# Residual stream kept transposed in two feed-forward stages of a fused macaron block

## The reference

```python
x = x + 0.5 * ffn(layernorm(x))
x = x + attn(layernorm(x))        # one head of 128, rotary, causal
x = x + 0.5 * ffn(layernorm(x))   # the same weights again

def ffn(xt):                      # xt: 8192 tokens x 128
    scores = sigmoid(xt @ gate_w.T)            # 16 experts
    idx = top_k(scores + gate_b, 4)
    w = 2.5 * scores[idx] / sum(scores[idx])   # comb: tokens x 16, zero elsewhere
    y = sum over e of comb[:, e] * (silu(xt @ g_e.T) * (xt @ u_e.T)) @ w2_e.T
    return y + (silu(xt @ g_s.T) * (xt @ u_s.T)) @ w2_s.T
```

## Time and profile before

| | before |
|---|---|
| median of 3 executions | 861.89 us (861.54 to 862.0) |
| profiled execution, own time | 863.0 us |
| span, first to last instruction | 861.2 us |
| PE busy | 844.4 us (98%) |
| DVE busy | 694.2 us (81%) |
| ACT busy | 591.2 us (69%) |
| POOL busy | 557.6 us (65%) |
| mean granted PE clock | 0.998 of full |
| HBM read and written | 74.92 MB, 5.24 MB |

### The profile page before, as it was taken

The page is one execution under the profiler, slowest core; times in us unless marked ns, Lnnn a source line. Parts: engine busy times, 40 slices in busy tenths (PEclk is TensorE's granted clock), DMA queues, the critical chain, the costliest instruction groups (busy, mean ns, idle before and its releaser), DMA issues.

```text
span 861.2 us, 18145 instructions
## 1 busy us (share of the span) xinstructions
PE 844.4 (98%) x4506; PEld 709.0 (82%) x4506; DVE 694.2 (81%) x2125; ACT 591.2 (69%) x1215; POOL 557.6 (65%) x519
## 2 busy tenths in 40 slices
PE   8999999999999999999999999999999999999998
PEld 7788888888888876889999998788888888888886
DVE  6888888888888887777776667788888888888885
ACT  5566666666666687777778866766666666666664
POOL 6666666666666678866767762466666666666664
PEclk9999999999999999999999999999999999999999
DMA  3684444455555341222111220445545444444553
GB/s 123 185 233 113 111 111 113 114 126 131 133 122 136 101 114 36 50 51 46 38 40 25 48 49 1 111 124 129 134 124 136 111 111 111 112 112 125 127 134 82
DMA packets 63494, 89.01 MB, mean 103 GB/s; under 512 B 7520, under 2 KB 26208, under 8 KB 63200
## 3 DMA queue, kind: packets, MB, share of 16 engines
q1 hardware_dynamic: 63456, 88.58, 41.3%
HBM read 74.92 MB, written 5.24 MB: 93 GB/s over the span
## 4 chain that ended last, share of the span: by engine, by line
PE 52%; ACT 4%; issue 2%; DVE 2%; POOL 1%; ACTq 0%; DVEq 0%; POOLq 0%
PE bank L1318 47%; PE bank L1628 3%; PE bank L1402 1%; PE bank L1423 1%; ACT prob L740 1%; ACT probT L551 1%; ACT xn L612 1%; ACT qkT L551 1%; ACT xh L551 0%; ACT xn L558 0%; POOL qkT L412 0%; DVE prob L933 0%; DVE X L1214 0%; DVE probT L943 0%; PE bank L1416 0%
## 5 line engine op out<-in xcount | busy, mean ns | idle before, releaser
L412 POOL TENSOR_TENSOR h_l<-probT,h_h 128x512 fp32r<-128x512 f32 x254 | 328.9, 1296 | 202.8 <-ACT h_h L551 202.7
L551 ACT ACTIVATE h_h<-probT 128x512 fp32r<-128x512 f32 (+1 forms) x286 | 179.5, 628 | 72.6 <-DVE probT L943 70.0
L1318 PE MATMUL bank<-xh,w_h 128*128 128x512 f32 x544 | 223.4, 411 | 2.0 <-DVE prob L933 1.9
L586 ACT ACTIVATE bank<-bank 128x512 f32<-128x512 f32 x252 | 146.2, 580 | 103.0 <-PE bank L1318 98.6
L1318 PE MATMUL bank<-xh,w_l 128*128 128x512 f32 x544 | 214.9, 395 | 0.0
L933 DVE TENSOR_TENSOR prob<-bank,qkT 128x512 f32<-128x512 f32 x252 | 173.5, 689 | 50.6 <-ACT bank L586 37.7
L1318 PE MATMUL bank<-xl,w_h 128*128 128x512 f32 x544 | 213.2, 392 | 0.0
L943 DVE TENSOR_TENSOR probT<-prob,bank 128x512 f32<-128x512 f32 x255 | 173.8, 681 | 12.7 <-DVE biased L874 5.0
L1318 PEld LDWEIGHTS bank<-xh,w_h 128*128 128x128 f32 x544 | 102.7, 189 | 23.9 <-DVE prob L933 2.7
L1318 PEld LDWEIGHTS bank<-xh,w_l 128*128 128x128 f32 x544 | 102.5, 188 | 23.9
L1318 PEld LDWEIGHTS bank<-xl,w_h 128*128 128x128 f32 x544 | 102.9, 189 | 19.5
(11 more groups left out here) (117 smaller groups left out, 1332.4 us busy)
## 6 DMA issues: line engine op xcount, KB each, us to landing
qkT<-comb_rows SPq DMA_DIRECT2D x190, 256.0 KB, 5.2
qkT<-comb_rows SPq DMA_DIRECT2D x124, 128.0 KB, 2.9
stage<-stage SPq DMA_DIRECT2D x64, 128.0 KB, 2.4
X<-in_x SPq DMA_DIRECT2D x16, 256.0 KB, 6.2
out_x<-X SPq DMA_DIRECT2D x15, 256.0 KB, 5.8
comb_rows<-combT SPq DMA_DIRECT2D x32, 32.0 KB, 1.8
cos<-in_cos SPq DMA_DIRECT2D x1, 1024.0 KB, 8.3
sin<-in_sin SPq DMA_DIRECT2D x1, 1024.0 KB, 10.7
```

The source lines that it names most:

```text
L412: nc.gpsimd.tensor_tensor(lo, f, hi.bitcast(F32), ALU.subtract).then_inc(done, 1)
L551: return nc.scalar.activation(dst, src, ACT.Copy)
L586: nc.scalar.activation(bank[:, G_BANK[g], :], bank[:, G_BANK[g], :], ACT.Silu).then_inc(silu_done, 1)
L1318: return nc.tensor.matmul(dst, lhsT, rhs, start=start, stop=stop)
```

## The change

The residual of both FFNs is kept transposed (features on partitions) in four buffers `xT`, a ring of 512 tokens each. In the first FFN they are loaded from a transposed copy `x_t` that the host gives; in the second they are made from the rows of `X` by four PE transposes and one ACT copy. The output leaves the kernel transposed and the host turns it. The rows of `X` are still loaded, for the statistics.

The minus mean and the inverse deviation of tile T+3 are written by POOL into two new rows of `comb`; they ride along with the transposition of `comb` and its trip through DRAM, and one more DMA repeats them over 128 partitions (`rows`). POOL adds the minus mean to `xT` (`ffn_center`, 128x512), DVE multiplies by the deviation into bank 7 (`ffn_scale`, 128x512), two tiles ahead. `ffn_xn` and `ffn_xnT` remain for the first two tiles of each FFN. The residual is added by DVE straight from the bank `Y` to `xT`; in the first FFN, PE transposes the sum and ACT copies it into `X` (`ffn_X`); in the second it is stored as it is. The loops have bodies of four tiles, and PE's loop of the second FFN is written out.

```diff
+RING = 4
+TURNS = TILES // RING
@@ SP
+            load(X[:, 2 * NB:3 * NB, :], x_v[:, 2 * NB:3 * NB, :], x_loaded[2])
             load(w13_f[:, early[2], :], w13T[:, early[2], :], w13_loaded[2])
             load(w2_f, w2T, w2_loaded)
-            load(X[:, 2 * NB:3 * NB, :], x_v[:, 2 * NB:3 * NB, :], x_loaded[2])
+            load(X[:, 3 * NB:4 * NB, :], x_v[:, 3 * NB:4 * NB, :], x_loaded[3])
+            for r in range(RING):
+                load(xT[r], x_t[:, TILE * r:TILE * (r + 1)], xT_moved[r])
...
+            def load_xT(T, r):
+                sp.wait_ge(y_ready, T - RING + 1)
+                sp.dma_start(xT[r], x_t[:, bass.ds(TILE * T, TILE)]).then_inc(xT_moved[r], 16)
...
+                if ahead:
+                    wait(sp, xs_done, scaled_count(T + 1, base))
+                    sp.dma_start(rows[:], comb_d[q, NEXP:NEXP + 2, :].rearrange("(a e) t -> a e t", a=1
+                                                                                ).to_broadcast([P, 2, TILE])
+                                 ).then_inc(rows_loaded, 16)
+            def store(T, r):
+                sp.wait_ge(xr_done, T + 1)
+                sp.dma_start(out_t[:, bass.ds(TILE * (T - TILES), TILE)], xT[r]).then_inc(xT_moved[r], 16)
...
+                    for c in range(RING):
+                        comb_rows(4 * k + 2 + c, c % 2)
+                        load_x(4 * k + 6 + c, c % 2)
+                        load_xT(4 * k + 4 + c, c)
...
+                    for c in range(RING):
+                        store(4 * k + TILES + c, c)
+                        comb_rows(4 * k + TILES + 2 + c, c % 2, 0, TILES)
@@ POOL
+            def ffn_rows(T, q):
+                at = slice(NB * q, NB * (q + 1))
+                pool.wait_ge(var_done, ln_count(T))
+                wait(pool, combT_ready, T - 2)
+                nc.gpsimd.tensor_tensor(comb[:, NEXP + 1, :], var_eps[:, at], neg_half[:, at], ALU.pow).then_inc(rstd_done, 1)
+                nc.gpsimd.tensor_tensor(comb[:, NEXP, :], mv[:, at, 0], neg_one[:, at], ALU.mult).then_inc(neg_mean_done, 1)
+            def ffn_center(T, base, turn, c):
+                n = scaled_count(T, base)
+                pool.wait_ge(rows_loaded, 16 * n)
...
+                wait(pool, xs_done, n - 1)
+                nc.gpsimd.tensor_tensor(xc, xT[c], rows[:, 0, :], ALU.add).then_inc(xc_done, 1)
...
-                    elif j == 2 and not last:
-                        ffn_rstd(T + 2)
+                    elif j == 2 and (t is None or t + 3 < TILES):
+                        ffn_rows(T + 3, 1 - q)
+                    if j == 3 and ahead:
+                        ffn_center(T + 2, base, turn + (c + 2) // RING, (c + 2) % RING)
@@ ACT
+            def ffn_xh(T, q, base):
+                act.wait_ge(gate_ready, UNITS * (T - 1))
+                act.wait_ge(xs_done, scaled_count(T, base))
+                copy(xh[q][:], bank[:, T_BANK, :]).then_inc(xh_done, 1)
+            def ffn_xT(T, turn, c):
+                act.wait_ge(xT_ready, turned_count(T))
+                act.wait_ge(xT_moved[c], 16 * turn)
+                copy(xT[c], bank[:, YT_BANK, :]).then_inc(xT_copied, 1)
+            def ffn_X(T, Tx):
+                act.wait_ge(y_ready, T + 1)
+                copy(X[:, tile_blocks(Tx), :], bank[:, YT_BANK, :].rearrange("p (n d) -> p n d", n=NB)).then_inc(x_done, 1)
...
                         ffn_silu(T, q, j)
+                    if j == UNITS - 1 and ahead:
+                        ffn_xh(T + 2, q, base)
...
-                    if j == LAG and not first:
-                        ffn_yT(T - 1, 1 - q)
+                    if base:
+                        if j == 0 and ahead:
+                            ffn_xT(T + 2, turn + (c + 2) // RING, (c + 2) % RING)
...
+                    elif j == PAIRS - 1 and not first:
+                        ffn_X(T - 1, T - 1)
...
-                    elif 0 <= at < NB and not last:
-                        ffn_xn(T + 2, Tx + 2, at)
@@ DVE
+            def ffn_scale(T, base):
+                dve.wait_ge(xc_done, scaled_count(T, base))
+                dve.wait_ge(combT_done, T)
+                nc.vector.tensor_tensor(bank[:, T_BANK, :], xc, rows[:, 1, :], ALU.mult).then_inc(xs_done, 1)
...
+                    nc.vector.scalar_tensor_tensor(xT[c][:, cols], bank[:, Y_BANK[c % 2], cols], 0.5, xT[c][:, cols],
+                                                   ALU.mult, ALU.add).then_inc(xr_done, 1)
...
                     ffn_h(T, q, j)
+                    if j == NB and not first:
+                        residual(T - 1, back)
...
                 ffn_weighted(T, q, PAIRS - 1)
-                if not first:
-                    residual(T - 1, Tx - 1)
                 ffn_h(T, q, PAIRS - 1)
+                    ffn_scale(T + 2, base)
...
                 ffn_h(T, q, PAIRS)
+                    ffn_xl(T + 2, q)
@@ DVE, ffn_start: between ln_apply and ffn_xl(0, 0), and after it
+                dve.wait_ge(x_loaded[1], 16)
+                ffn_stats(1, 1, 1)
+                ffn_stats_wait(1)
+                ffn_mv(1, 1)
+                ffn_var(1, 1)
                 ffn_xl(0, 0)
+                dve.wait_ge(x_loaded[2], 16)
+                ffn_stats(2, 2, 0)
@@ PE
+            def ffn_y(T, c):
+                pe.wait_ge(xr_done, T + 1)
...
+                    ins = nc.tensor.transpose(bank[:, YT_BANK, n * P:(n + 1) * P], xT[c][:, n * P:(n + 1) * P], ident[:])
+            def ffn_xT(T, Tx):
+                pe.wait_ge(attn_done, QB * (Tx // 2 + 1))
+                wait(pe, xT_copied, turned_count(T) - 1)
...
-                if not last:
+                if first:
                     ffn_xnT(T + 1)
+                if base and (t is None or t + 2 < TILES):
+                    ffn_xT(T + 2, T + 2 - base)
...
-                    if j == 4 and not first:
+                    elif j == 6 and not first:
...
+                if start:
+                    with pe.Fori(0, TURNS - 1) as k:
+                        for c in range(1, RING + 1):
+                            ffn_tile(base, k + c // RING, c % RING)
+                else:
+                    for t in range(1, TILES - LAG):
+                        ffn_tile(base, turn + t // RING, t % RING)
```

More of the change, by code:

```diff
@@ L223, in macaron @@
         neg_shift_done = sem("neg_shift_done")
+        rows_loaded = sem("rows_loaded")
+        xc_done = sem("xc_done")
+        xs_done = sem("xs_done")
+        xT_ready = sem("xT_ready")
+        xT_copied = sem("xT_copied")
         xn_done = sem("xn_done")
@@ L425, in ffn_tile @@
+            def ffn_tile(base, turn, c, first_batch=None):
+                T, q = RING * turn + c, c % 2
+                last, t = False, None
+                if isinstance(T, int):
+                    t = T - base
+                    last = t == TILES - 1
+                ahead = t is None or t + 2 < TILES
                 for j in range(UNITS):
@@ L622, in comb_spread, with ffn_tile @@
                                                            ).to_broadcast([P, NB, 2, INTER])).then_inc(spread_copied, 1)
-            def ffn_tile(T, Tx, q, first, last, first_batch=None, start=False):
+            def ffn_tile(base, turn, c, first_batch=None):
+                T, q = RING * turn + c, c % 2
+                first, last, t = False, False, None
+                if isinstance(T, int):
+                    t = T - base
+                    first, last = t == 0, t == TILES - 1
+                start = first and base == 0
+                ahead = t is None or t + 2 < TILES
                 for j in range(UNITS):
@@ L630, in ffn_tile @@
                             attn_hi(FIRST_HI[j], 0, 0)
-                    if j == 0 and not last and not start:
-                        ffn_xh(T + 1, 1 - q)
+                    if j == 0 and first and not start:
+                        opening_xh(T + 1, 1 - q)
                     if j == (7 if start else 6) and not last:
@@ L995, in ffn_tile @@
+            def ffn_tile(base, turn, c, first_batch=None):
+                T, q = RING * turn + c, c % 2
+                first, last, t = False, False, None
+                if isinstance(T, int):
+                    t = T - base
+                    first, last = t == 0, t == TILES - 1
+                start = first and base == 0
+                stats_next = t is None or t + 3 < TILES
+                N, L, Lx, back = T + 1, T + 3, T + 3 - base, (c - 1) % RING
                 if start:
```

420 lines of the change are left out of this document (212 added, 208 removed).

## The result

The changed kernel takes 872.76 us (median; 868.94 to 875.63) where the kernel before takes 861.71 (861.41 to 862.0): ratio 1.0121, 95% interval 1.0105 to 1.0137. It is slower by 11 us; 850.0 was predicted, faster by 12. Two things are in the trace: leaving out what four tiles take too long, the span is shorter by 11.7 us, near the 12.1 predicted; and in these four tiles something that I had given a chance of 0.05 took 17.65 in the profiled execution and some 21 in the middle one.

A forecast was written before the change was run, and what follows sets the result against it. PE, never idle in the FFNs, was taken as the bound. From 861.9 us, transposes -12.2, start +1.1 and end -1.0 sum to -12.1, so 849.8, rounded to 850.0; range 847.0 to 854.2.

The forecast's parts named there:

- the longer loop bodies stall: Rival: four-tile bodies cost an instruction fetch at each of four jumps back, 0 to 12 us, middle 856; chance 0.05.
- Price of the transposes: PE in the FFNs: 0.45 us a group of four transposes, net 27 groups gone, 12.2 us less (11.6 to 12.4).
- DVE at the tile's end: DVE's new scale, 0.68 us, replaces the residual in the end-of-tile cluster; 1.4 us of cover, cost nothing, bound 0.3 a tile.
- the match-replace row: DVE's two-SBUF-input operation in the loop: 160 to 171 ns in all 128 executions, read as no blocking by POOL.
- POOL: POOL in each tile: centering adds 1.29 us, moves the low half of unit 4 by 0.4; covered with 1.2 left.
- DMA: FFN tile loads: `rows` and `xT` land at about 146.5, cover about 1.8 us; likely no cost, up to 1 us once.
- the rival at 879: Rival: the DMA queue becomes the bound, `rows` or `xT` landing late in every tile; 879 us, chance 0.05.
- the one at 858: Rival: DVE's chain at the tile's end passes its 1.4 us by 0.3, 8 us over 27; 858 us, chance 0.07.
- Start: Kernel's start: DVE makes tile 1's statistics before `xl` of tile 0, +1.1 us (ends 0 and 1.4).
- The half-clock stretch: Near the start, PE at 1.2 GHz for some 3.5 us; 1.3 us either way if it vanished or came twice.
- End: Kernel's end: DVE reads `Y` itself, SP issues the store about 0.98 earlier, -1.0 us (0.5 to 1.0).
- Attention: Between the FFNs: extra statistics on DVE, a copy moved from DVE to ACT; 0, bounds -0.5 and +0.5.

The follow-up runs named there:

- experiment 7: Changed kernel, four-tile loops kept, with 110 one-cell memsets on DVE ahead of its first wait for x: 870.34 us, ratio 1.0086.
- experiment 4: Kernel of experiment 1 with each group of four transposes through bank 4 issued twice: 861.12 us, ratio 0.9985 to the kernel before.
- experiment 1: Changed kernel with only DVE's two FFN loops written out (the written-out version, without jumps): 851.3 us against 862.5, ratio 0.9867.
- experiment 11: Kernel before plus, behind all its work, DVE probes of 128x512 in three operand forms, POOL idle then busy: 0.62 us alone, 1.69 and 1.66 beside POOL with two SBUF inputs.
- experiment 2: Kernel before with DVE's loop bodies of four tiles instead of two, leftover tiles written out: 875.29 us, ratio 1.0161.
- experiment 6: Kernel before, DVE's two-tile body padded by 66 one-cell memsets a tile (348 and 347 instructions): 877.52 us, one execution.
- experiment 5: Kernel before, DVE's two-tile body padded by 36 one-cell memsets a tile (288 instructions in the first FFN): 862.06 us, one execution.
- experiment 3: Changed kernel, second FFN's loop loads of comb_b bringing 128 of 512 columns: 869.17 us, one execution.
- experiment 8: Changed kernel with 110 one-cell memsets on DVE behind the first FFN's loop, so only the second loop moves: 870.12 us, ratio 1.0098.
- experiment 9: Kernel of experiment 6 with 88 one-cell memsets ahead of DVE's first wait for x: 892.24 us, one execution.
- experiment 10: Kernel of experiment 6 with 44 one-cell memsets ahead of DVE's first wait for x: 907.87 us, one execution.

## Why the prediction was wrong

**The step that failed** is that the sum puts the four jumps back at nothing: it has no term for them, and they took 17.65 us. They stood only in the rival "the longer loop bodies stall". Its mechanism and place were right (four jumps, gaps on one engine at every fourth tile) and its chance of 0.05 had no reason behind it. I had the row that bears on it: one packet in 140 us, and as many on the other queue, says that bodies of this length are not reloaded. It says nothing of twice the length. My count was loose too: "52 instructions in 20 us" are the records; the stream holds 433 for four tiles, 108 a tile.

**Its price was short as well**, by what follows PE's idle time. I took 4.9 us a fetch less 1.9 of cover, 12 at most. The fetch was near: 17.7 / 4 = 4.4 us. So was the cover: DVE's four waits of 5.77, 4.72, 2.59 and 4.58 us left PE idle for 4.32, 3.27, 0.79 and 2.73, 11.1 in all, so 1.45 to 1.85 of each was covered. But the four tiles are longer by 17.65, 6.5 us more than that, and this took back what the cover had given. Of it, 3.4 us come from the clock: behind the idle times of 4.32 and 3.27 PE ran for 3.4 us each at the 1.2 GHz level, where half of the time is lost (9 matmuls in 3 us where the next 3 us have 14). At the other two jumps the clock stayed at 1.00 and the tiles still lost 1.4 us each behind the idle time; there PE's matmuls start up to 0.62 us apart. DVE, with 18.65 of 20 us busy even where no jump disturbs it (written out, 640 to 660 us), has little spare time in which to catch up what it is late; that this is the reason is argued, not tested.

The other executions of the changed kernel are slower (median 872.8, profiled 868.9), at a mean granted clock of 0.987 to 0.990 where the profiled one has 0.996. They have no trace, but that of experiment 7 is of that kind (873.64 us): four waits of 18.5 in all, and behind the jumps some 13.6 us at granted clock 0.50, in three stretches, where the changed kernel's trace has 6.8. Together this makes the 21 us between 872.8 and 851.3.

**Price of the transposes:** 0.45 a group predicted, 0.42 by experiment 4, and 0.45 from tile to tile (19.74 to 19.29) in experiment 1. Over both stages -11.2 where -12.2 was the sum. Two of the tiles at the ends of the first stage (19.53, 19.70) are longer than the rest.

**DVE at the tile's end:** the scale was priced at 0.68 and takes 1.11 on average; it was the term where the Trainium skill's rule ("SBUF — State Buffer", section "Who interferes with whom") and the match-replace row spoke against each other, and experiment 11 shows the contention (1.66 to 1.69 us beside POOL, 0.62 alone). The row misled perhaps because its operands are small; no run varied their size. It cost nothing in the tile, since the slot had the 1.4 us of cover, and the tiles between jumps are 19.27 to 19.33, as forecast (19.3).

**POOL:** the centering takes 1.31 (1.29 predicted), waits 1.9 us for `rows` at its first tile and 0.6 for the transposed input, and nowhere else. **DMA:** a load of `rows` lands 7.2 us after its issue; no queue bound. Both covers held, and neither the rival at 879 nor the one at 858 came about.

**Start:** +1.15 us to the first `combT` (1.1 predicted). The half-clock stretch behind it, put in the range as 1.3 either way, went away: the second gap is 17.82 against 19.39. About 1.0 of that isn't the change's doing: experiments 2, 6 and 11, whose start is that of the kernel before, have 18.38 there, without a half-clock stretch. **End:** the first half of DVE's last operation starts at 864.01 and SP issues at 864.46, and the last group of `combT` is 1.49 us nearer to the end (1.0 predicted).

```profile
864.01 0.75 DVE L1077 SCALAR_TENSOR_TENSOR stage<-bank,stage 128x256 f32<-128x256 f32 x2 [0.66 <-PE bank L1434]
864.46 0.82 SPq L417 DMA_DIRECT2D out_x_t<-stage  x2
```

**Attention:** 0 predicted with 0.5 either way, +1.4 measured (+1.6 written out). The view of POOL's waits between 300 and 335 us has one long wait in it, for the swap of halves in the first batch's rotary step; first before, then after:

```profile
POOL rope_s L502 <- DMA stage<-stage: 2.3, 1, 2.3
```

```profile
POOL rope_s L572 <- DMA stage<-stage: 3.8, 1, 3.8
```

POOL's low half stands behind it and PE behind that. The gap across the attention less this wait is 229.8 before, 229.7 after, 229.9 written out (3.8 there too), 230.3 in experiment 4 (1.2) and 229.5 in experiment 5 (1.7): the wait is most of the difference. SP issues the swap behind the ten loads of `comb_b`, and those behind the DMA that writes `comb`:

```profile
315.16 0.31 SPq L361 DMA_DIRECT2D comb_rows<-combT  x1
318.48 6.28 SPq L366 DMA_DIRECT2D qkT<-comb_rows  x10
325.12 4.26 SPq L424 DMA_DIRECT2D stage<-stage  x4
```

From the first to the second issue it is 3.3 us after, 3.0 written out, 1.8 before and 1.5 in experiment 4. It is 3.0 to 3.4 in experiments 3, 7 and 8 too. Why that one small DMA took longer in these kernels is open. A single instruction packet on q8 lay beside it in each of them and none in the other two, but no run tested that.

**The forecast without the jumps:** taking the four excesses out of the profiled execution leaves 868.94 - 17.65 = 851.3, which is 11.7 less than the 863.0 of the profiled execution before, where 12.1 was the sum. The terms are off by more than their sum: transposes +1.0, attention +1.4, against -1.6 behind the start and -0.5 at the end. That they cancel is luck in part. The kernel without the jumps measures 851.3, 11.2 less than the 862.5 measured beside it; that the two figures of 851.3 agree to the decimal is chance, since one comes from the fastest execution and the other is a median (its own profiled execution took 853.45, with two half-clock stretches near its start).

## What to carry to other kernels

When a change makes a hardware loop's body longer, count the body in the compiled stream, waits and register instructions included, and look in the profile for instruction packets while a loop turns: none means that it fits, some a turn means that each jump back waits for them. On DVE here 288 instructions ran, 348 ran or stalled with their start, 433 stalled at every jump; written out, the loop ran without a wait. When you price a stall on an engine with 90% of its time used, take the cover off, but put on what follows: here, behind 11.1 us of TensorE's idle time, 6.5 more, half of it lost at 1.2 GHz.

## What the runs showed of the hardware

- Instruction packets on DVE's queue are 8.2 KB, 128 instructions. All kernels here fit an engine that keeps three of them: bodies of 215, 226 and 288 instructions never stalled, 424 to 435 always did, 347 and 348 stalled or not as 0, 44 or 88 instructions ahead of them shifted their start. Three is inferred from these patterns, not seen. The patterns alone would also allow smaller steps (six of 64, for one); that the step is 128 rests on the size of the packets.
- A jump back out of reach costs DVE 2.6 to 5.8 us in the changed kernel, up to 6.4 with the loops moved (experiment 7), 3.3 to 3.8 at most in experiments 2, 6, 9 and 10, and in the last two a second wait of up to 3.8 us further on in the same turn.
- Read straight on, the same engine's instructions (2920 in the written-out version) loaded with no wait.
- The other instruction queue moved 16 KB packets, 8 of them from 590 to 810 us both in the changed kernel and written out; in the written-out version no tile there was longer for it. Which engine they serve was not tested.
- Two SBUF inputs on DVE beside POOL at work in SBUF: 1.66 to 1.69 us for 128x512 in place of 0.62, and 0.62 with one input in PSUM.
